# Node degrees as four stretches of columns in four column groups of TensorE, and a second small product that spreads their reciprocals over the partitions

## The reference, cut to what matters

```python
xn = _batchnorm(x, norm1_g, norm1_b)
msg = xn[edge_index[0]]
agg = jax.ops.segment_sum(msg, edge_index[1], num_segments=N)
deg = jax.ops.segment_sum(jnp.ones((E,), x.dtype), edge_index[1], num_segments=N)
agg = agg / jnp.maximum(deg, 1.0)[:, None]
conv_out = jax.nn.relu(agg @ W_conv + b_conv)
```

## Time and profile before

| | |
|---|---|
| median of 3 runs | 365.79 us (365.54, 365.79, 367.07) |
| the profiled execution's own time | 365.55 us |
| its span in the trace | 363.7 us |
| TensorE busy | 348.0 us, 96% |
| VectorE busy | 246.4 us, 68% |
| ScalarE busy | 181.3 us, 50% |
| mean granted clock of TensorE | 0.998 |

### The profile page before, as it was taken

One profiled execution on the slowest core, in us unless ns is written; L12 is line 12 of the kernel. 1 busy time (PEld: TensorE's weight loads), 2 busy tenths in 40 slices (PEclk: granted clock), 3 DMA queues, 4 the chain that ended last, 5 costly groups with the idle time before them and its releaser, 6 DMA issues.

```text
span 363.7 us, 6194 instructions
## 1 busy us (share of the span) xinstructions
PE 348.0 (96%) x2072; PEld 224.0 (62%) x2072; DVE 246.4 (68%) x667; ACT 181.3 (50%) x302; POOL 95.2 (26%) x163
## 2 busy tenths in 40 slices
PE   7899899989999999999998999999999999999994
PEld 3678655757777666767564675455555555565562
DVE  5889999998998995867998787522464443422325
ACT  0548538768477167454437766411534645233132
POOL 8132120000000000100042778722277465101100
PEclk9999999999999999999999999999999999999999
DMA  6990303300000000034900000000000000010223
GB/s 162 289 303 30 119 1 119 118 3 1 3 3 4 3 3 3 3 97 148 264 9 3 0 2 3 2 2 1 2 0 0 2 0 2 0 51 21 70 58 85
DMA packets 13539, 18.05 MB, mean 50 GB/s; under 512 B 1839, under 2 KB 6895, under 8 KB 13491
## 3 DMA queue, kind: packets, MB, share of 16 engines
q1 hardware_dynamic: 12538, 17.21, 16.4%
q10 hardware_dynamic: 953, 0.23, 0.3%
HBM read 14.88 MB, written 2.56 MB: 48 GB/s over the span
## 4 chain that ended last, share of the span: by engine, by line
PE 74%; DVE 15%; issue 4%; ACT 3%; DVEq 2%; DMA 0%; POOL 0%; SPq 0%; ACTq 0%; POOLq 0%
PE bank L1424 71%; DVE ring L988 2%; DVE st L1095 2%; DVE st_row L938 2%; PE bank L1815 1%; PE bank L1454 1%; PE bank L1774 1%; ACT hn L688 1%; DVEq L1137 1%; DVE st_row L1310 1%; DVE x L1305 1%; DVE mv_row L939 1%; DVE x L1375 0%; PE bank L1635 0%; DVE ln_tmp L933 0%
## 5 line engine op out<-in xcount | busy, mean ns | idle before, releaser
L1424 PE MATMUL bank<-AT,hh 125*128 125x400 f16 (+3 forms) x250 | 81.2, 332 | 1.2 <-DVEq L1335 0.4
L1424 PE MATMUL bank<-AT,hl 125*128 125x400 f16 (+3 forms) x250 | 80.9, 332 | 0.0
L988 DVE TENSOR_SCALAR ring<-iota_code,code 125x250 f16<-125x250 f16 x200 | 46.1, 307 | 1.4 <-issue 1.4
L1424 PEld LDWEIGHTS bank<-AT,hh 125*128 125x128 f16 x250 | 24.1, 97 | 19.8 <-issue 1.1
L1424 PEld LDWEIGHTS bank<-AT,hl 125*128 125x128 f16 x250 | 24.2, 97 | 17.6 <-issue 0.2
L1424 PE MATMUL bank<-ring,S 125*128 125x250 f16 x200 | 33.5, 310 | 0.0
L1424 PE MATMUL bank<-a_hi,w_hi 128*128 128x400 f16 (+1 forms) x96 | 32.6, 340 | 0.0
L1424 PE MATMUL bank<-agg_hi,w_hi 128*128 128x400 f16 (+1 forms) x96 | 32.6, 339 | 0.0
L1424 PE MATMUL bank<-agg_hi,w_lo 128*128 128x400 f16 (+1 forms) x96 | 32.5, 339 | 0.0
L1424 PE MATMUL bank<-a_hi,w_lo 128*128 128x400 f16 (+1 forms) x96 | 32.5, 339 | 0.0
L1424 PE MATMUL bank<-agg_lo,w_hi 128*128 128x400 f16 (+1 forms) x96 | 32.5, 339 | 0.0
(11 more groups left out here) (229 smaller groups left out, 703.0 us busy)
## 6 DMA issues: line engine op xcount, KB each, us to landing
w_s<-w SPq DMA_DIRECT2D x4, 1024.0 KB, 5.2
x_in<-x SPq DMA_DIRECT2D x5, 448.0 KB
x<-x SPq DMA_DIRECT2D x2, 1120.0 KB
out<-x SPq DMA_DIRECT2D x6, 224.0 KB
wB<-wk SPq DMA_DIRECT2D x1, 1024.0 KB, 9.6
wA<-wq SPq DMA_DIRECT2D x1, 1024.0 KB, 13.8
wC<-w_conv SPq DMA_DIRECT2D x1, 1024.0 KB, 16.1
wB<-wv SPq DMA_DIRECT2D x1, 1024.0 KB, 6.3
```

Source lines behind the costliest of these rows:

```text
L988: return dve.tensor_scalar(ring[:, slot, j, a:b], iota_code[0:CH, a:b], code[:, bass.ds(c + j, 1)], float(-CODES * t), ALU.subtract, ALU.i ...
L1424: return pe.matmul(o, l, r, start=start, stop=stop, skip_group_check=True)
```

## The change

D computes each degree once in place of 128 times. The block's columns are cut in four stretches of 113 (450 columns) or 100 (400 columns). Each stretch is summed by its own products with an all-ones matrix of 125x32, into partitions 0 to 31, 32 to 63, 64 to 95 and 96 to 127 of the bank, that is in the four column groups. That makes 40 products in place of 10. VectorE reads the bank, and does its two operations on 128x113 or 128x100 into a new tile `rdq`. A new group `Ec` spreads it: four products in 32-bit floats, each with a column of the identity matrix, broadcast to 128x128, as the stationary operand and `rdq` as the moving one, so that stretch g lands on all 128 partitions of the bank at its columns. ScalarE copies that bank to `rdb` for all three blocks. `mean_rows` waits for this copy (`s_rdb`).

D0 and D1 move one slot ahead (to 17 and 22), E0 and E1 stand in the slots in which D0 and D1 stood, D2 moves to the front of `LAST`, and E2 stands behind A02, the first sum of the last block. The banks of `LAST` are dealt anew.

```diff
-    "MX2 G8", "QT2 G9", "KV2 UK3 D0", "O2 UQ3 A00", "A10", "MX3 A20", "QT3 A30 F1", "KV3 D1 A01",
+    "MX2 G8", "QT2 G9 D0", "KV2 UK3 E0", "O2 UQ3 A00", "A10", "MX3 A20", "QT3 A30 F1 D1", "KV3 E1 A01",
...
-LAST = "A31 F2 D2 A02 A12 A22 A32 A33".split()
+def quarters(c):
+
+    c0, w = COLS[c]
+    q = -(-w // 4)
+    return [min(g * q, w - q) for g in range(4)], q
...
+LAST = "D2 A31 F2 A02 E2 A12 A22 A32 A33".split()
...
-LAST_BANKS = (6, 4, 0, 1, 2, 3, 7, 5)
+LAST_BANKS = (0, 6, 4, 1, 5, 2, 3, 7, 0)
...
+        rdq = place("rdq", [P, -(-COLS[0][1] // 4)], F32, 152)
...
-                if name[0] == "D":
-                    free_group(copy(rdb[:, c0:c0 + w], ps[:, 0:w]), name)
+                if name[0] == "E":
+                    act.activation(rdb[:, c0:c0 + w], ps[:, 0:w], ACT.Copy).then_inc(sem("s_rdb"), 1)
+                    act.wait_ge(sem("s_rdb"), c + 1)
+                    act.sem_inc(free[PLACE[name][0]], 1)
...
             weight_mean(1)
+            counts_out("E2")
...
                 elif name[0] == "D":
-                    c0, w = COLS[int(name[1])]
+                    c = int(name[1])
+                    d = rdq[:, 0:quarters(c)[1]]
                     dve.wait_ge(sem("s_bn1"), 1)
-                    d = rdb[:, c0:c0 + w]
-                    if name in LAST:
-                        ps = read_group(dve, name)[:, 0:w]
-                    else:
-                        dve.wait_ge(free[PLACE[name][0]], PLACE[name][1] + 1)
-                        ps = d
+                    ps = read_group(dve, name)[:, 0:quarters(c)[1]]
+                    if c:
+                        dve.wait_ge(full[PLACE[f"E{c - 1}"][0]], PLACE[f"E{c - 1}"][1] + 1)
                     own.step(dve.tensor_scalar(d, ps, 1.0, wscale[:, 0:1], ALU.max, ALU.mult))
-                    n_deg[0] = own.mark(dve.reciprocal(d, d))
-                    if name in LAST:
-                        dve.sem_inc(free[PLACE[name][0]], 1)
+                    dve.reciprocal(d, d).then_inc(sem("s_rdq"), 1)
+                    dve.sem_inc(free[PLACE[name][0]], 1)
...
-                own.after(n_deg[0])
+                dve.wait_ge(sem("s_rdb"), ci + 1 if ci < NC else NC)
...
-                    ins = accumulate([(ps[:, 0:w], [(ones16[0:L, :], AT[:, k, c0:c0 + w]) for k in range(T)],
-                                       [(ones16[0:L, :], ATlo[:, k, c0:c0 + w]) for k in range(T)])])[0]
+
+                    starts, w = quarters(int(name[1]))
+                    places = [ps[g * 32:(g + 1) * 32, 0:w] for g in range(4)]
+                    blocks = [slice(c0 + s, c0 + s + w) for s in starts]
+                    ins = sum_up([[(o, ones16[0:L, 0:32], AT[:, k, b]) for o, b in zip(places, blocks)] for k in range(T)],
+                                 [(o, ones16[0:L, 0:32], ATlo[:, k, b]) for k in range(T) for o, b in zip(places, blocks)])
+                elif name[0] == "E":
+                    c = int(name[1])
+                    starts, w = quarters(c)
+                    pe.wait_ge(sem("s_rdq"), c + 1)
+                    ps = open_group(pe, name)
+                    for g, s in enumerate(starts):
+                        ins = mm(ps[:, s:s + w], ident[:, 32 * g:32 * g + 1].broadcast_to([P, P]), rdq[:, 0:w], True, True)
```

More of the change, by code:

```diff
@@ L765, in _ @@
                         conv_high(int(name[1]))
-                    elif name[0] in "AD":
+                    elif name[0] in "AE":
                         counts_out(name)
+                    elif name[0] == "D":
+                        pass
                     else:
@@ L1056, in attention @@
                     dve.sem_inc(free[PLACE[name][0]], 1)
-            n_deg = [0]
             def weight_low(layer, half):
@@ L1682, in accumulate, with sum_up @@
                 return last
+            def sum_up(steps, extra):
+                for o, l, r in steps[0]:
+                    mm(o, l, r, True, False)
+                with pe.If_lt(big_r, most_r):
+                    for o, l, r in extra:
+                        mm(o, l, r, False, False)
+                pe.end_ifs()
+                for n, step in enumerate(steps[1:]):
+                    for o, l, r in step:
+                        ins = mm(o, l, r, False, n == len(steps) - 2)
+                return ins
             seen = pe.alloc_register("seen")
```

## The result

The changed kernel takes 370.54 us (median of five runs, 369.80 to 371.42). The kernel before takes 365.79 us beside it. The ratio is 1.0128, with a 95% interval of 1.0113 to 1.0143: 4.7 us slower, where 0.2 us slower was forecast. The profiled execution took 370.98 us with a span of 369.2 us, 5.5 us more than before.

A forecast was written before the change was run, and what follows sets the result against it. TensorE, busy for 96% of the span, was taken to bound the kernel up to 188.88 us. Block terms 0.40 - 0.82 + 0.24 = -0.18 us made it 0.2 us slower: median 366.0 us, 8-in-10 range 365.1 to 367.4 us.

The forecast's parts named there:

- E0: First block's spreading group on TensorE: reached at 118.17 us, after VectorE is done at 117.71 us, so no wait; 0.88 us.
- a fixed tail: After 188.88 us: what follows starts from the last block of A32 and A33 and was taken as fixed.
- in these prices: On TensorE: the 114 records more, 90 for D and 24 for E, were taken as covered by the prices of D and E.
- for what I have not seen: The chance of 0.05 left over for causes outside the forecast and its rivals.
- D side by side: In the three D groups: the four column groups run side by side, 0.63 us for D0 and 0.58 us for D1 and D2.
- for entering and leaving: In each D group: 0.13 us on top of its products, taken from the group N0.
- Rival C: In the D groups: products of different column groups run one behind the other; 3.3 us slower, 369.1 us; chance 0.09.
- B: In the D groups: side by side, but products cannot be issued fast enough, about 1.1 us a D; 367.0 us; chance 0.2.
- E: On TensorE: each E group's four 32-bit products take 0.88 us, 2.64 us of new work for the three.
- First block: At D0 and E0: 1.91 us of old D0 replaced by 0.63 and 0.88 us, without a wait; gain 0.40 us.
- Second block: At D1 and E1: TensorE waits 0.9 us for VectorE's `rdq` before E1, which ends at 149.36 us; loss 0.82 us.
- Third block: At D2 and E2 in `LAST`: 1.70 us replaced by 0.58 and 0.88 us, without a wait; gain 0.24 us.

The follow-up runs named there:

- kernel 1: The kernel before with 78 never-executed products added to the skipped branches of the 13 aggregates: 369.92 us against 365.86 us, ratio 1.0117.
- kernel 2: The changed kernel with 64 never-executed products more, half a block of instructions: 366.61 us beside 365.86 us for the kernel before, ratio 1.0020.
- a_pad128: The changed kernel with 128 never-executed products more, a whole block of instructions: 370.08 us beside 365.86 us for the kernel before, ratio 1.0124.
- b_pad74: The kernel before with 74 never-executed products added to the skipped branches of the aggregates: 366.83 us against 365.60 us, ratio 1.0028.
- kernel 4: The changed kernel with the one jump over 120 skipped products cut into ten jumps over 12: 366.63 us, ratio 1.0035 to the kernel before.
- kernel 7: The kernel before with 78 never-executed products and the long jump cut into ten short ones: 366.17 us beside 366.03 us, ratio 1.0002.
- kernel 9: The changed kernel with 64 never-executed products, D1 ahead of A20 in slot 21, and E1 in bank 2: 365.74 us beside 366.03 us for the kernel before.
- Kernel 8: The changed kernel with 64 never-executed products and D1 ahead of A20 in slot 21, bank 7: 366.22 us beside 365.60 us for the kernel before.

## Why the prediction was wrong

**The step that failed.** "Behind that point comes a fixed tail": I ended the account at 188.88 us and took what follows as a constant to be shifted. The tail runs the same operations, but it depended on where the program's instructions lie. I had even written down the 114 records more and found them "in these prices". Their price was at a jump 39 us behind. Of the 5.35 us, 1.57 us are the pause and 2.75 us the clock behind it. Kernels 1 to 3 and 5 show that the place of the jump modulo 256 makes the pause, and kernel 1 that the degrees have no part in it but their instruction count. That it is a fetch which comes too late is the reading that fits the places, the packets and kernels 4 and 7; the profile names no releaser. None of the four rivals was of this kind. Only the 0.05 "for what I have not seen" was.

**D side by side** held. D costs 0.55 or 0.56 us where an aggregate's product follows (171.47, and 133.99 in kernel 9), as forecast with 0.58 us. It costs 0.77 and 0.78 us where the counts of a window follow. Between them stands the register load of the window's bounds, which a queue of 80 short instructions may no longer hide. That is argued, not shown. The forecast's 0.13 us for entering and leaving was to cover the way in too, and that comes on top: the group in front of D0, D1 and D2 takes 0.09, 0.07 and 0.10 us longer than in the kernel before. The 1.0 us estimated from the Trainium skill's figure ("TensorEngine Tiling (Array Packing)", section Performance Considerations) does not appear: 40 products took 0.55 us, 14 ns each, against the estimate's 25 ns. Rival C (1.9 us a D) is out. So is B's 1.1 us, though D0 and D1 with the way in (0.87 and 0.84 us) stand midway to it.

**E** costs 0.98, 0.94 and 0.87 us, against 0.88 us. E0 has 113 columns in place of 100 and is also the only one that a window's counts follow; no run tells which of the two makes it 0.1 us dearer. E1 costs 0.92 us in kernel 9, where it does not wait, so of the 0.1 us taken for the exposed first load only 0.02 us shows.

**First block**: forecast gain 0.40 us, measured 119.45 - 119.43 = 0.02 us. There was no wait. The loss is in D0 (0.78 us, and 0.09 us more in front of it than G9's pitch, against 0.63 us) and in E0 (0.1 us).

**Second block**: forecast loss 0.82 us with A01 at 149.36 us. Measured: A01 at 149.35 us, a loss of 0.83 us from the place that the first block left. VectorE was done at 148.32 us, as forecast, but TensorE came late. By KV3's pitch of 1.74 us in kernel 9 it was through at 145.95 + 1.74 = 147.69 us instead of 147.42 us, for D1 is 0.19 us dearer and 0.07 us longer in front. So it stood for 0.72 us, of which the row shows 0.57 us, since idle time counts only from the modelled end of KV3's last product. D1's extra time fell into the wait and cost nothing. The reason given for it was half of it: "KV3's copy would hold bank 6 for E1 as well, but ends earlier". With D1 ahead of it KV3 came later, and the copy ended at 148.27 us and not 148.02 us. Kernel 8 shows that the copy alone holds E1 as long, and kernel 9 that both have to go.

**Third block**: forecast gain 0.24 us. The lateness falls from 0.81 us at A01 to 0.66 us at 189.63 us, a gain of 0.15 us. The parts give about as much: 1.69 us for the old D2, less 0.55 us, 0.10 us in front and 0.87 us. No wait before E2, as forecast.

**The sum** at 189 us is 0.66 us in place of 0.18 us. Kernels 2 and 4, which have this part alone, measured 0.75 and 0.77 us over the kernel before beside them. Without the pause the median would have lain inside the range. Of the error of 4.5 us, 0.5 us are the three blocks, most of it D0's price, and the rest is the tail.

## What to carry to other kernels

When a change adds or removes instructions on an engine, count them up to every long skipped stretch behind it. A jump over nearly a block of 256 instructions, from beside one edge to just before the next, cost 1.45 to 2.43 us here and mostly a fall of the clock. This kernel fell into it and out of it by shifts that change no executed product. Cutting the skipped stretch into short ones took the pause away at the one place modulo 256 that was tried, and cost nothing measurable in the kernel before. When a timing surprises, look first at whether the lost time lies where the edit is, and test a bare shift before explaining the edit.

A group that waits for two engines gains nothing when one of them gets earlier. Ask of each wait what else holds it, the bank's last user above all.

## What the runs showed of the hardware that was not expected

The pause was 2.00, 2.43 and 2.42 us where four products stood between landing and edge, and 1.45 us with eight. The clock fell to the lower level behind two of the three long pauses that were profiled, and not behind the third (`a_pad128`, 2.42 us, clock 1.00 behind it). By the mean clock of the other executions (0.995 or less, against 0.996 or more) it fell in twelve of the thirteen of these kernels, and in none of the ten of `b_pad74`. Why it sometimes stays is open.

Both kernels have one more pause without a releaser, unchanged by the edit. In the changed kernel, TensorE's row and one of VectorE's:

```profile
78.94 0.40 PE L1434 MATMUL bank<-wC_hi,hn_hi 128*125 128x512 f16 x1 [1.58 <-issue]
78.16 0.68 DVE L1113 TENSOR_TENSOR hn_lo<-hn,hn_hi 128x500 f16<-128x500 f32 x1
```

This one is of another kind. The group is G3, and the program makes it wait for the third `hn_lo` of VectorE (`s_hns`), which ends at 78.16 + 0.68 = 78.84 us, 0.1 us ahead of it. TensorE's instruction fetches start at 71.01 and 81.37 us, none in between. So "issue" in a profile can also be a wait whose releaser it does not name, and the program's own waits are to be looked at first.
